# A graph network's edge layer on one core: the source part of an item by four products of 192 columns in place of twelve of 64

## The reference, cut to what matters

```
pair = concatenate([x[src], x[dst]], axis=-1)          # one row of 128 per edge
h = relu(pair @ W1 + b1)                               # W1 [128, 64]
interaction = h @ W2 + b2
gate = sigmoid(interaction @ Wg + bg)
gated = interaction * gate
summed = segment_sum(gated, src, num_segments=6250)
pooled = summed / maximum(counts, 1)
x = layernorm(x + pooled)
```

## Time and profile before

| | |
|---|---|
| median of 3 executions | 4956.5 us (4948.54 to 4956.79) |
| the profiled execution's own time | 4944.84 us |
| its span, first to last instruction | 4943.1 us |
| TensorE busy | 3806.8 us, 77% |
| TensorE's weight loads busy | 3226.9 us, 65% |
| VectorE busy | 2378.4 us, 48% |
| ScalarE busy | 1739.9 us, 35% |
| GpSimd busy | 1589.3 us, 32% |
| mean granted TensorE clock | 0.685 of full |

### The profile page before, as it was taken

One profiled execution on the slowest core, in us unless ns is written; L12 is line 12 of the kernel. 1 busy time (PEld: TensorE's weight loads), 2 busy tenths in 40 slices (PEclk: granted clock), 3 DMA queues, 4 the chain that ended last, 5 costly groups with the idle time before them and its releaser, 6 DMA issues. The chain is left out here.

```text
span 4943.1 us, 130898 instructions
## 1 busy us (share of the span) xinstructions
PE 3806.8 (77%) x40671; PEld 3226.9 (65%) x40672; DVE 2378.4 (48%) x7074; ACT 1739.9 (35%) x3888; POOL 1589.3 (32%) x1694
## 2 busy tenths in 40 slices
PE   6872688888798989948777777778777777777776
PEld 3442344444498988947777777777777777777775
DVE  9998899999602121143333333333333333333335
ACT  7861588888500000022222222222222222222222
POOL 0000200000000000055555555555555555555553
PEclk9985799999899999955555555555555555555555
DMA  1000122222598888721111111111111111111111
GB/s 39 4 2 9 62 104 104 104 107 112 194 346 303 322 298 309 269 47 42 39 39 40 39 39 41 40 39 41 39 41 39 39 41 39 40 41 40 39 39 31
DMA packets 182945, 444.91 MB, mean 90 GB/s; under 512 B 53003, under 2 KB 111635, under 8 KB 157039
## 3 DMA queue, kind: packets, MB, share of 16 engines
q1 hardware_dynamic: 131583, 387.99, 22.8%
q0 software_dynamic: 51040, 53.55, 5.2%
q10 hardware_dynamic: 144, 1.05, 0.1%
HBM read 356.29 MB, written 86.12 MB: 90 GB/s over the span
## 5 line engine op out<-in xcount | busy, mean ns | idle before, releaser
L1109 POOL DMA_INDIRECT x<-b_table,gidx x1568 | 1488.7, 949 | 1245.3 <-DVE x L930 808.3
L1412 ACT ACTIVATE x<-ps,b1col 64x256 f32<-64x256 f32 x880 | 411.9, 468 | 1725.6 <-remote 1525.4
L1766 PE MATMUL ps<-w2cat,x 65*128 65x128 f32 x3520 | 855.3, 423 | 17.1 <-issue 16.0
L1778 PEld LDWEIGHTS ps<-x 128*128 128x128 f32 x3520 | 804.8, 333 | 35.5 <-issue 23.3
L1778 PE MATMUL ps<-x 128*128 128x65 f32 x3520 | 800.2, 404 | 30.8 <-issue 21.5
L1766 PEld LDWEIGHTS ps<-w2cat,x 65*128 65x128 f32 x3520 | 800.0, 331 | 32.2 <-issue 19.8
L1746 PE MATMUL ps<-x 128*128 128x64 bf16 x5280 | 467.9, 239 | 439.6 <-issue 422.4
L930 DVE TENSOR_TENSOR x<-ps,x 128x256 f32<-128x256 f32 x440 | 186.9, 425 | 1245.4 <-remote 707.2
L1746 PEld LDWEIGHTS ps<-x 128*128 128x128 bf16 x5280 | 417.4, 138 | 512.3 <-issue 511.2
L1574 PE MATMUL ps<-rows 128*128 128x448 bf16 x2272 | 616.9, 399 | 148.5 <-DVE rows L715 71.7
L1574 PEld LDWEIGHTS ps<-rows 128*128 128x128 bf16 x2272 | 328.9, 145 | 436.3 <-issue 309.9
(11 more groups left out here) (271 smaller groups left out, 2639.5 us busy)
## 6 DMA issues: line engine op xcount, KB each, us to landing
rows<-adjacency SPq DMA_DIRECT2D x90, 1024.0 KB, 5.1
adjacency<-stage SPq DMA_DIRECT2D x50, 1568.0 KB, 5.2
x<-adjacency SPq DMA_DIRECT2D x60, 1024.0 KB, 5.4
x<-src_rows SPq DMA_DIRECT2D x440, 128.0 KB
rows<-adjacency SPq DMA_DIRECT2D x90, 544.0 KB, 4.8
x<-adjacency SPq DMA_DIRECT2D x60, 544.0 KB, 5.5
x<-b_table,gidx POOLq DMA_INDIRECT x1568
key_rows<-x ACTq DMA_DIRECT2D x1, 1024.0 KB, 4.4
```

The source lines that it names most:

```text
L1109: e.indirect_dma_start(out=BGT[:, s, j, :], out_offset=None, in_=b_table, in_offset=bass.IndirectOffsetOnAxis(ap=gidx[:, u * G + j:u * G + ...
L1412: ins = e.activation(pair[:, :, h, :], ps[h * D:(h + 1) * D, u, 0:2 * P].rearrange("p (a n) -> p a n", n=P), ACT.Relu, bias=b1col[h * D:(h ...
L1766: ins = e.matmul(ps[:, 2 + u, j * P:(j + 1) * P], H[0:D + 1, u, j * P:(j + 1) * P], w2cat[:], start=True, stop=True)
L1778: ins = e.matmul(ps[:, 4 + u, 0:D + 1], OS[:, s, j, :], MG[:, u, j, :], start=(j == 0), stop=(j == G - 1))
```

## The change

`edge_rows` makes one product per column j, with all 192 columns of `AT` as its moving side. The three parts of a result then stand side by side in PSUM, in 192 columns; two columns j share a bank, and the item takes banks 6 and 7 both. So there is one set of PSUM columns for all items, and `edge_rows(i)` waits for `parts_summed` of item i - 1. `add_b` first sums the three parts on VectorE, with two reductions (one bank each) that read each group of three values 64 columns apart and write `BT`, then waits for the second of them, and then adds the gathered rows to `BT` in place. `b_added` is counted up by that last addition as before. Everything else is unchanged.

```diff
+        parts_summed = sem("parts_summed")
...
                 e.wait_ge(rows_ready, i + 1)
                 e.wait_ge(groups_landed, g)
-                e.tensor_tensor(BT[:, s, :], ps[:, 6 + s % 2, 0:G * D],
+                for h in range(2):
+                    three = ps[:, 6 + h, 0:6 * D].rearrange("p (j k f) -> p j f k", j=2, k=3)
+                    ins = e.tensor_reduce(BT[:, s, h * P:(h + 1) * P].rearrange("p (j f) -> p j f", j=2), three, AX_X,
+                                          ALU.add)
+                ins.then_inc(parts_summed, 1)
+                e.wait_ge(parts_summed, i + 1)
+                e.tensor_tensor(BT[:, s, :], BT[:, s, :],
                                 BGT[:, bass.ds(slot, 1), :, :].rearrange("p s j f -> p (s j f)"), ALU.add
                                 ).then_inc(b_added, 1)
...
                 if not first:
-                    e.wait_ge(b_added, i - 1)
+                    e.wait_ge(parts_summed, i)
                 for j in range(G):
-                    for k in range(3):
-                        ins = e.matmul(ps[:, 6 + s % 2, j * D:(j + 1) * D], OT[:, s % 2, j * P:(j + 1) * P],
-                                       AT[:, s, k * D:(k + 1) * D], start=(k == 0), stop=(k == 2))
+                    at = j % 2 * 3 * D
+                    ins = e.matmul(ps[:, 6 + j // 2, at:at + 3 * D], OT[:, s % 2, j * P:(j + 1) * P],
+                                   AT[:, s, :], start=True, stop=True, skip_group_check=True)
                 ins.then_inc(rows_ready, 1)
...
-                edge_rows(i, i % 4, i < 2)
+                edge_rows(i, i % 4, i < 1)
```

## The result

The changed kernel took 5167.83 us (median of 4, 5137.66 to 5187.3) against 4952.52 us of the kernel before: ratio 1.0433, 95% interval 1.0409 to 1.0457, +215 us. The forecast was 5245 us. The profiled execution took 5182.78 us, its span 5181.1 us, so profile against profile it is +238 us.

A forecast was written before the change was run, and what follows sets the result against it. It took a closed loop of add, gathers and slow stretch as the bound: 224 + 77 + 10 = +311 us, less 5% +295 us, hence 5240 to 5250 us, forecast 5245 us; 8-in-10 range 5080 to 5430 us.

The forecast's parts named there:

- stretches: 440-item loop: during gather bursts, until 1.8 us after the last gather, TensorE creeps and ScalarE stands, up to 8.8 us.
- Products, sums, add: Per item: product group 0.64 to 0.66 us; two reductions 1.13 us; add unchanged, at most 0.36 us longer beside GpSimd's gathers.
- The wait for parts_summed: VectorE's wait for its own reductions before the add: 0.03 us, like chained instructions elsewhere in the trace.
- TensorE's wait for parts_summed: TensorE's edge products wait for the previous item's reductions, so the turn is later: counted as nothing, upper bound 0.3 us.
- VectorE's own pace: VectorE's unhindered round grows from 3.43 to 4.6 us, over TensorE's 4.42; 49 items needing no new slot cost 10 us.
- In the loop: Add-and-gather turns: 1.16 us of reductions before the add, 193 times, 224 us; 0.4 us later next add each, 77 us.
- bursts of eight: GpSimd's eight gathers in a row, refilling two ring slots a turn; their disappearance would show the prediction wrong.
- Hopping reads: Rival, 13%: VectorE's reductions, reading at a step of 64 values, take 0.47 us longer each, +180 us: 5430 us.
- Short bursts: Rival, 12%: a second add over 5.0 us behind the first leaves GpSimd dry after four gathers, +124 us: 5080 us.
- Creeping products as the end of the chain: Rival, 9%: release waits for TensorE's edge products, so 16 fewer instructions save 280 us: 4680 us, or 4790 us.
- Hidden: Rival, 5%: the reductions fall into VectorE's idle time, TensorE's pace decides and nothing moves: 4955 us.
- The reading that no hopping read of the trace is slow: Sort's L561, said to step two words: all 570 compares, 417 to 1228 ns, show no penalty against 1220 for 1024 values.

The follow-up runs named there:

- the sums alone: Kernel before plus the two reductions and their wait ahead of the add, result overwritten, twelve products and both bank sets kept: ratios 1.0198 and 1.0205.
- one bank set: Kernel before with edge_rows(i) waiting for b_added of item i - 1 instead of i - 2, no reductions added: ratios 1.0008 and 1.0007.
- the products without the sums: Changed kernel with its four 192-column products, but VectorE adds only the first part straight from PSUM; edge_rows(i) waits for b_added of item i - 1: 0.997.
- the sums ahead of the loads: Changed kernel with VectorE's two reductions moved before add_b's two register loads: ratio 1.0098 on a 5024.05 us chip, 1.0005 on a 4147.25 us chip.
- the run with the landing awaited first: Kernel before with GpSimd waiting for a group's rows to land ahead of the next group's first gather, not its fourth: 4981.61 us, ratio 0.9921.

## Why the prediction was right, and where it was not

Direction and size held: +215 us measured, +293 us forecast (5245 - 4952), inside the range. The cause that was named first, VectorE's sums, held too: the sums alone cost as much as the whole change where there are no stretches, and without them the cost is gone where there are. But the terms of the sum do not describe what happened, and that the time came out near it is in part luck: on the other chip with stretches the same code cost 48 us, while the range's lower end, 5080 us, stands for some 125 us.

- *Products, sums, add.* Close: product group 0.6 to 0.7 us, sums 553 ns (552 worked out), add 426 ns. But the two sums overlap, 1.02 us together where 1.13 us was put down. The upper bound for the add, from GpSimd's company, did not come into play: 462 ns was the longest of 440.
- *The wait for parts_summed* was put at 0.03 us; it is 0.17 us (70.8 us in 425 waits), 0.14 us more in every item. The chain of the earlier trace rows has fixed addresses; this add takes its ring slot from a register, and the sequencer's step for that (81 ns, median of 440, on L937) comes behind the wait. That this is the difference was not tested. Sums and wait together are 3601.81 - 3600.62 = 1.19 us, beside the 1.16 us put down; the two errors nearly cancel.
- *TensorE's wait for parts_summed* at nothing: shown right without stretches, by one bank set (1.001) and by the sums alone costing the whole. With stretches the wait is there (388 us in 192 waits), but a longer one in the products without the sums (677 us) went with a ratio of 0.997.
- *VectorE's own pace* was worked out as 4.6 us and is 4.59 us between two items, 4.64 us on the mean. It was charged to the 49 items that need no new slot, 10 us. Without stretches it is charged to all: (4.64 - 4.46) x 440 = 79 us of the 83 us measured. With stretches it is not: the sums ahead of the loads take this pace away, and gained 2 us there, give or take 20.
- *In the loop* is the step that failed. The two terms, 224 + 77 us, took two things as fixed. The first is the number of turns (193): 170 waits of GpSimd remain, and bursts of eight fell from 166 to 100, which was named as a sign of being wrong and came in part. The second is that VectorE stands just before its add at a release: in more than half of the cases it does not (71 of 122, as at 3521.34), and the add then comes by several us later than the 1.16 + 0.4 us put down. So there are fewer and costlier turns, and the balance differs from chip to chip, +215 us and +48 us. Which part each has in the +215 us was not measured. The 83 us of pace can't be taken off them to find the loop's part, since moving the sums gained nothing on the chip with stretches where it was tried.
- *Rivals.* Hopping reads: refuted for these reads out of PSUM, 545 to 559 ns at a step of 64 values, the rate of a contiguous read. The Trainium skill's table (Vector Engine (DVE) Microarchitecture Reference, "Measured stream behaviour on trn2") is of SBUF ports; these reads are from PSUM, and its factor of 1.6 does not carry over to them. Short bursts: came in part, 89 bursts of four; what they gave back was not measured. Creeping products as the end of the chain: refuted at its price of 280 us by the products without the sums (0.997). Hidden: refuted in both kinds of chip.
- *The reading that no hopping read of the trace is slow* is wrong, though nothing of the sum hangs on it. It holds for the sort's step of two words (512 values in 684 to 694 ns, as at other steps). But its first stage compares at a step of four words, and these four instructions take 0.3 us more than the next eight of the same size, which read neighbours or words two apart (VectorE, L561, at 24.3 to 27.6 and 27.7 to 31.8 us):

```profile
L561 DVE TENSOR_TENSOR x<-x x4: 869/882/893, 24.4 to 26.8; 128x400 f32<-128x400 f32 x4
```

```profile
L561 DVE TENSOR_TENSOR x<-x x8: 569/570/577, 27.7 to 31.2; 128x400 f32<-128x400 f32 x8
```

  The longest duration of all forms together, 1228 ns, could not show that. In these four the hop costs some 0.3 us / 400 = 0.75 ns a value; GpSimd worked beside them, but also beside the first of the next eight. The sums, which read PSUM, show nothing like it.
- The page's rule on VectorE's modes fits here: the Trainium skill (VectorE: DVE Perf Modes, "The perf-mode tier table (the rule you actually need)") lists `tensor_reduce` with a 1x mode only, and the trace agrees, 384 values in 553 ns, 1.04 ns a value behind the fixed part of the earlier trace rows.

**Open.** What causes the slow stretches, in which the sequencers crawl while gathers follow one another without a pause (in the one of the earlier trace rows, three steps of VectorE's sequencer for L952 to L954 take 0.70 to 0.71 us each; steps of the same kinds outside it take 0.02 to 0.19 us), and why some chips lack them. What one bank set alone, or the sums alone, cost on a chip that has them: both met only chips without. Why the same change costs 4.3% on one such chip and 0.9% on another.

## What to carry to other kernels

An engine that idles for a third of the time can still be the pace of a loop, as VectorE is in the changed kernel without stretches (1145 us busy of 1700 us):

```profile
2300.00:4000.00 1700.00, 1660.74 (x8043) 1550.61 (x8042) 1145.03 (x3657) 615.61 (x1462) 1259.62 (x1326) 0.50 0.23 54
```

Add up its own round with register loads and waits, compare it with the bound's, and where no stall holds the loop, charge the difference to every item. New work on such an engine can be free if it is put where the engine only waits for its own sequencer, here ahead of the register loads: 1.020 became 1.0005 with the same instructions, on a chip without stretches. And a cost that rests on an unexplained stall should be measured on more than one chip.

## What the runs showed of the hardware that was not expected

The kernel before takes 4142 to 4147 us on some chips and 4952 to 5024 us on others, some 20%, with the same instructions. The granted clock in this stage is 0.50 in the profiles from both kinds. On the faster kind TensorE is busy all the time (1688 of 1700 us in the kernel with one bank set, whose time is that of the kernel before there):

```profile
2300.00:4000.00 1700.00, 1688.61 (x11405) 1682.92 (x11405) 821.89 (x3040) 640.47 (x1522) 1283.43 (x1361) 0.50 0.23 56
```

There GpSimd gathers in unbroken bursts of over a hundred (of 224 more than once), and no wait of ScalarE or VectorE is put down to `remote`; so unbroken bursts alone do not make a slow stretch. That one is needed is suggested by the run with the landing awaited first, in which 24 of 184 unnamed waits before L1412 were left, but is not shown.
